# Forming part of the one-hot tiles of an edge-counting stage on ScalarE

## The reference, cut to what matters

```python
N = 1250                       # nodes, 512 features each
src, dst                       # 41250 edges, sorted by dst
sums = jax.ops.segment_sum(beta[dst], src, num_segments=x.shape[0])      # first layer
counts = jax.ops.segment_sum(jnp.ones_like(src, dtype=beta.dtype), src, num_segments=x.shape[0])
neigh_sum = jax.ops.segment_sum(x[edge_src], edge_dst, num_segments=n)   # third layer
```

## Time and profile before

| | us |
|---|---|
| median of 3 runs | 1569.64 |
| lowest and highest of them | 1569.23, 1570.88 |
| the profiled execution, its own time | 1569.58 |
| span of its trace | 1567.8 |
| edge tiles in the span (first and last hot_m) | 13.1 to 133.7 |
| next stage starts | 137.9 |

### The profile page before, as it was taken

How to read it: one execution, slowest core, us unless ns; L and a number is a source line. 1 busy time by engine, 2 the same in 40 slices (tenths; PEclk the granted TensorE clock), 3 DMA queues, 4 the chain that set the end, 5 groups by cost and what they waited for, 6 DMA issues and landing times. The chain is left out here.

```text
span 1567.8 us, 22143 instructions
## 1 busy us (share of the span) xinstructions
PE 1451.7 (93%) x8144; PEld 898.9 (57%) x8144; DVE 963.7 (61%) x1779; ACT 721.3 (46%) x1406; POOL 611.4 (39%) x502
## 2 busy tenths in 40 slices
PE   5888999999898899999999899889999988997998
PEld 3554545447777654454556544546676776775664
DVE  7998254326666411123123323768999999999994
ACT  5542114336666410110111230256777887888783
POOL 4887200040645200000000060017786785785863
PEclk8999999999999989999999999989999999999999
DMA  7001000054242240000000200003020110101001
GB/s 249 1 2 85 0 0 1 0 145 101 52 77 52 75 179 0 0 1 0 0 0 1 81 0 0 1 17 78 10 58 3 35 30 5 35 11 25 1 1 66
DMA packets 37915, 58.04 MB, mean 37 GB/s; under 512 B 17056, under 2 KB 21796, under 8 KB 37552
## 3 DMA queue, kind: packets, MB, share of 16 engines
q1 hardware_dynamic: 36496, 54.05, 12.9%
q10 hardware_dynamic: 1312, 2.56, 0.4%
HBM read 31.06 MB, written 5.87 MB: 24 GB/s over the span
## 5 line engine op out<-in xcount | busy, mean ns | idle before, releaser
L1525 POOL TENSOR_TENSOR tl_ex<-tl_ex,tl_left 128x1250 f32<-128x1250 f32 x80 | 209.7, 2621 | 28.9 <-ACT tl_left L1860 24.2
L1344 DVE SCALAR_TENSOR_TENSOR X<-ex_ps_x,g,X 128x512 f32<-128x512 f32 x80 | 59.9, 751 | 192.6 <-PE ex_ps_x L1237 192.6
L1665 PE MATMUL tl_banks<-identf,tl_ex 128*128 128x128 f32 x800 | 134.4, 283 | 23.6 <-ACT tl_pt L1881 14.0
L2029 POOL TENSOR_TENSOR lo<-xn,hi 128x512 f16<-128x512 f32 x5 | 5.9, 1186 | 373.0 <-ACT hi L2133 373.0
L1881 ACT COPY tl_pt<-tl_banks 128x512 f32<-128x512 f32 (+1 forms) x200 | 108.1, 541 | 91.2 <-PE tl_banks L1665 90.7
L1210 PE MATMUL ex_ps_h<-yt,w 128*128 128x512 f32 (+1 forms) x384 | 144.5, 530 | 0.0
L1237 PE MATMUL ex_ps_x<-w,hid 128*128 128x512 f32 (+1 forms) x320 | 143.1, 599 | 0.0
L1290 ACT ACTIVATE hid<-ex_ps_h,b 128x512 f32<-128x512 f32 (+1 forms) x48 | 29.1, 608 | 242.6 <-PE ex_ps_h L1210 242.6
L1665 PEld LDWEIGHTS tl_banks<-identf,tl_ex 128*128 128x128 f32 x800 | 89.0, 141 | 84.9 <-issue 44.4
L1951 DVE MAX8 tl_m<-tl_banks 128x8 f32<-128x1250 f32 x80 | 116.3, 1453 | 10.1 <-PE tl_banks L1635 9.9
L1957 DVE MAX8 tl_m<-tl_left 128x8 f32<-128x1250 f32 x80 | 117.1, 1464 | 2.8
(11 more groups left out here) (283 smaller groups left out, 2952.4 us busy)
## 6 DMA issues: line engine op xcount, KB each, us to landing
tl_kl<-tl_KT SPq DMA_DIRECT2D x16, 320.0 KB, 4.4
tl_qs<-tl_QO SPq DMA_DIRECT2D x16, 320.0 KB, 5.7
kl<-KT SPq DMA_DIRECT2D x14, 320.0 KB, 4.2
qs<-QO SPq DMA_DIRECT2D x14, 320.0 KB, 5.8
w<-in_L_ffn_W SPq DMA_DIRECT2D x8, 512.0 KB
w<-in_L_ffn_W SPq DMA_DIRECT2D x4, 1024.0 KB, 8.9
at_kept<-AT SPq DMA_DIRECT2D x1, 3200.0 KB, 9.0
AT<-at_kept SPq DMA_DIRECT2D x1, 3200.0 KB, 18.7
```

What stands on the lines that cost most here:

```text
L1525: pool.tensor_tensor(ex[:, n % EXS, 0:N], ex[:, n % EXS, 0:N], left[:, n % LEFT, :], ALU.subtract).then_inc(s_probs, 1)
L1665: mm = pe.transpose(ps_t[:, b * P:(b + 1) * P], ex[:, n % EXS, a + b * P:a + (b + 1) * P], m.identf[:, :])
```

## The change

From tile ACT_FROM = 45 on, `hot_b` of the tiles with t % 5 of 0 and t % 8 not 0 (`by_act`, 49 tiles: 45, 50, 55, 60, 65, 70, 75, 85, ...) is made by ScalarE instead of VectorE, in two instructions: |b - ruler| into a small buffer `apart`, then relu(1 - that), which is one where the difference is 0, and 0 elsewhere, since both are whole numbers. ScalarE does it at the loop's head ACT_AHEAD = 5 tiles ahead, before the other jobs of that tile.

```diff
+ACT_FROM = 45
+ACT_AHEAD = 5
+    by_act = [t for t in range(ACT_FROM, ET) if t % HOTS and t % 5 == 0]
+    def same_slot(written, t):
+
+        return sum(1 for v in written if v <= max([v for v in written if v < t and v % HOTS == t % HOTS], default=-1))
+        apart = space("apart", 148608, [P, 2, P], F16)
...
                 if by_pool.index(t):
                     pool.wait_ge(s_half_hot, by_pool.index(t))
+                if same_slot(by_act, t):
+                    pool.wait_ge(s_act_hot, same_slot(by_act, t))
...
-                    one_hot(t % HOTS, None if t in by_pool else ends[:, 0, t:t + 1], ends[:, 1, t:t + 1], WIN * NT)
+                    one_hot(t % HOTS, None if t in by_pool or t in by_act else ends[:, 0, t:t + 1], ends[:, 1, t:t + 1], WIN * NT)
...
+                    if t in by_act:
+                        pe.wait_ge(s_act_hot, by_act.index(t) + 1)
...
             act.wait_ge(s_zeroed, 1)
+            act.wait_ge(s_made, 10)
...
+            def act_hot(t):
+                v = by_act.index(t)
+                act.wait_ge(s_used, used[t - HOTS])
+                act.wait_ge(s_half_hot, same_slot(by_pool, t))
+                if v >= 2:
+                    act.wait_ge(s_act_hot, v - 1)
+                act.activation(apart[:, v % 2, :], m.ruler[:, 0:P], ACT.Abs, scale=-1.0, bias=ends[:, 0, t:t + 1]
+                               ).then_inc(s_apart, 1)
+                act.wait_ge(s_apart, v + 1)
+                act.activation(hot_b[:, t % HOTS, :], apart[:, v % 2, :], ACT.Relu, scale=-1.0, bias=m.ones[:, 0:1]
+                               ).then_inc(s_act_hot, 1)
+
             for t in range(ET):
+                if t + ACT_AHEAD in by_act:
+                    act_hot(t + ACT_AHEAD)
```

More of the change, by code:

```diff
@@ L137, in graph_in @@
         (s_made, s_zeroed, s_blank, s_edges, s_nodes, s_small, s_wc, s_base, s_split, s_flag, s_keyed, s_cols,
-         s_lined, s_flagged, s_onehot, s_half_hot, s_used, s_closed, s_drained, s_flipped, s_kept, s_shift, s_mean, s_var, s_inv,
+         s_lined, s_flagged, s_onehot, s_half_hot, s_apart, s_act_hot, s_used, s_closed, s_drained, s_flipped, s_kept, s_shift, s_mean, s_var, s_inv,
          s_scaled, s_rows, s_high, s_low, s_side, s_side_kept) = s.signals(
-            "made zeroed blank edges nodes small wc base split flag keyed cols lined flagged onehot half_hot used closed "
+            "made zeroed blank edges nodes small wc base split flag keyed cols lined flagged onehot half_hot apart act_hot used closed "
             "drained flipped kept shift mean var inv scaled rows high low side side_kept")
```

## The result

The changed kernel takes 1574.99 us (median), the kernel before, run beside it, 1570.68; the ratio is 1.002, with a 95% interval of 1.0011 to 1.003. The ratio makes it about 3.1 us more, the two medians 4.3. One of the changed kernel's twelve executions, in a slow state, took 3757 us and is left out of the ratio. The profiled execution of the changed kernel took 1572.83 us with a span of 1571.0; all rows of "after" are of that one.

The account below looks back on a forecast made before the run. The prediction took GpSimd, as full as VectorE, to bound the loop: -2.8 (slots) - 1.5 (quicker one-hots) + 1.3 (ScalarE) + 0.9 (third signal) = -2.1 us, from 1569.58 to 1567.5, range 1561.0 to 1573.0.

Parts of the forecast that it names:

- the second rival: In the loop, TensorE comes to wait for ScalarE's one-hots and xn: slower, +5.5 us, 1575.1; chance 0.19.
- GpSimd as the bound: In the loop, GpSimd is as full as VectorE and the later one, so only a small gain; chance 0.52.
- the rival with VectorE as the pace: VectorE sets the loop's pace, so its 49 one-hots' time is gained in full: -8.1 us, 1561.5; chance 0.14.
- Quicker one-hots on GpSimd: GpSimd's one-hots in the loop speed up with less VectorE work beside them: -1.5 us, bounds 0 and -2.8.
- GpSimd's 2.8 us without a slot: Loop time in which GpSimd could have worked but had no free slot, taken to go: -2.8 us, or 0.
- ScalarE, +1.3: Cost of ScalarE's added work in the loop: 1.1 for late one-hots, 0.2 for flips and turned rows; bounds 0.6 and 4.7.
- a quarter of it passes: Of 4.7 us of late one-hots, a quarter delays GpSimd, which lacked a free slot 22 of 93 times: +1.1.
- The pair, 0.68 us: ScalarE's two steps for one tile take 0.68 us; 0.47 from copies, 0.80 with more for the wait.
- The third signal on GpSimd, +0.9: An added wait before GpSimd's one-hots, 95 times, always long given, at 0.01 us each: +0.9 us.
- Marks that came true: Forecast signs: GpSimd's mean near 0.73, VectorE waiting some 12 us for TensorE, 49 hot_b records fewer, 98 ScalarE records.
- Marks that failed: Forecast signs: last hot_m some 2 us earlier, GpSimd's idle nearly all its own last one-hot, ScalarE records of 0.37.

Follow-up runs that it names:

- e1_relief: The changed kernel with the 49 one-hots left out altogether, made by neither VectorE nor ScalarE and waited for by nobody: 1569.64 us, 0.9977 of the kernel before.
- e7_for_pool: The changed kernel with ScalarE making 27 of GpSimd's one-hots and VectorE making all its own again: 1568.13 us, 0.9975 of the kernel before.
- e19_pool_relief: GpSimd relieved of 27 one-hots that nobody writes, no work added on ScalarE, VectorE as in the kernel before: 1568.41 us, 0.9976 of the kernel before.
- e2_beside: The kernel before with ScalarE's 49 two-step jobs added, slot waits included, written to a buffer nobody reads: 1577.67 us, 1.0039 of the kernel before.
- e13_no_slots: The kernel before with ScalarE's 49 two-step jobs written to a buffer nobody reads, without waits for a slot: 1577.35 us, 1.0025 of the kernel before.
- e12_again: The changed kernel run once more, unaltered, beside other kernels: 1574.22 us, 1.0017 of the kernel before.

## Why the prediction was wrong

The forecast was -2.1 us, 1567.5; measured is +3.1 in the first comparison and +2.7 in the second. Against the kernel before of the same session that is just inside the range's upper end of +3.4; the time of 1574.99 is 2 us above its end of 1573.0. About half of these 2 us are that the kernel before itself read 1.1 more than the 1569.58 that I started from, the rest that the two medians are 4.3 apart where the ratio says 3.1. The outcome is the side of the second rival (slower, 0.20), at a little over half its price.

- **GpSimd as the bound: right as against VectorE alone.** e1_relief gave -3.6 where the two gains of the sum were -2.8 and -1.5 and the rival with VectorE as the pace said -8.1. e7_for_pool and e19_pool_relief show it from the other side, and also how close VectorE is behind: 27 one-hots less, 20 us of GpSimd's work, brought only 3.8. On 91 of 97 tiles GpSimd was the later one in the trace of after.
- **Quicker one-hots on GpSimd: right in kind, too small.** I took 0.047 us for each of 33, 1.5 us. Measured: 40 ns on each of GpSimd's 93 in e1_relief, 3.7 us, and 48 ns in the change. That is above the bound of 2.8, and about half of the 8.1 of VectorE's time that went. The Trainium skill (SBUF — State Buffer, Who interferes with whom) has one engine block the other for a whole instruction when VectorE is in a two-port mode; by that rule, as the prediction worked it out, all 8.1 would come back, and no run here shows more than about half.
- **GpSimd's 2.8 us without a slot: wrong in the change.** By the same working (25.4 less 83 waits of 0.167) they are 11.5 us, and in e1_relief 4.7. They did not go, they grew, because TensorE gives slots back later. In the change +8.7 of slots, less 4.5 for quicker one-hots, make +4.2, beside 3.4 at the next stage's start.
- **ScalarE, +1.3: this step failed.** Two parts of it. I charged 1.1 for late one-hots, a quarter of 4.7; the 4.7 came as worked out (TensorE idle for 4.7 and 5.4 us before them, on 10 and 11 tiles instead of 9), and what part of it passes isn't measured apart. I gave 0.2 for flips and turned rows that wait for ScalarE; this was the large miss: e2_beside, where no one-hot can be late, puts the cost of the pairs at 6.1, e13_no_slots at 3.9. The rule "a quarter of it passes" was taken from how often GpSimd lacked a slot before, and in the change it lacked one twice as often (42 waits for TensorE, 22 before): the share is itself changed by the delay. I had moved each pair into ScalarE's timeline, but asked only when the one-hots would come, and not when the jobs behind them would.
- **The pair, 0.68 us: a little small.** Where two follow each other they start at 35.80 and 36.53 and the next job at 37.26, so one occupies the row for 0.73; from start to end it is 0.83 (78.69 to 79.52 above). 49 x 0.05 is 2.5 us more of ScalarE's time.
- **The second rival** named the right engine and both places where it is late, the one-hots (4.7) and `xn` in six of ten rounds (4.2). Its test was that GpSimd's idle time stays or grows, which it did, and that TensorE waits over 5 us for ScalarE's hot_b: 2.2 by the profile's row, 4.7 and 5.4 paired off over the stage, so just at the mark. What it left out is that late `xt` and `AT` copies cost as well, and that the cost doesn't need a late one-hot at all.
- **The third signal on GpSimd, +0.9: not seen.** Its waits for its own last one-hot are 4.2 us in 27, 0.156 each, 0.167 before (before 5 other one-hots the profile names ScalarE's signal, 1.6 us, and before 9 nobody, 1.4); e1_relief and the change differ by no more than ScalarE's part explains.
- **Marks that came true:** VectorE waits 13.5 us for TensorE ("some 12"), 49 and 98 records, no more table loads, GpSimd's mean fell, to 0.70 ("near 0.73"). Marks that failed: the last hot_m came 3.2 us later, not 2 earlier; GpSimd's idle time was not nearly all its own last one-hot, but 4.2 of 25.4; ScalarE's records took 0.40, not 0.37.

## What to carry to other kernels

An engine that is idle half the time has not half its time to give: if it works in order and others wait for its small jobs, find out how late each of those jobs may be, not only how late the new one may be. A cheap test is to give it the new work with the result thrown away; here that cost 6.1 us, while half as much work cost nothing. And when two engines are near their limit, ask what each piece of moved work takes off which of them: the same pair took 0.75 us off GpSimd or 0.165 off VectorE. Relieve one only until the other takes over.

## What the runs showed of the hardware

- A 128x128 ScalarE activation with a bias for each partition takes 0.40 us here (399 and 402 ns in the mean), and the next job starts 0.09 before its recorded end if it does not wait for it (79.43 above), 0.03 behind it if it does (79.12). The Trainium skill (ScalarE: Activation LUTs, What ACT_TABLE_LOAD costs) has a fixed part and a part for each column for such an instruction; an estimate from its figures is 387 ns. The nearest row before, 374, was further off.
- TensorE's granted clock can fall to half for some 7 us in one execution of a kernel and not in another (rows of after and of e12_again above). What stood ahead of the fall differs too little between them to name a cause.
- The next stage takes back a part of the delay: in the kernel before its first matmuls ran at half clock and took 0.59 us, after the change they ran at full clock and took 0.38. Before:

```profile
137.95 0.59 PE L712 MATMUL ca_banks<-A,hi 128*128 128x512 f16 x1 [1.68 <-PEq L135]
```

and after:

```profile
141.38 0.38 PE L739 MATMUL ca_banks<-A,hi 128*128 128x512 f16 x1 [1.68 <-PEq L142]
```

That was worth 1.5 us of the 3.4 in this pair of traces, and later stages differ by nearly as much again in the other direction. In the trace of e12_again the lag of 1.8 us was 0.2 after ten matmuls of the next stage and 4.5 at the last one, though nothing behind the first stage was changed: of a change of 3 us, a single pair of executions tells the place and not the size.
